# Merging the first self attention, the sign layer and the masked cross attention of a two-layer Perceiver kernel into one program, with batch 0 running ahead

## What is computed

```python
x = x + xattn0(layernorm(x), ctx)      # 16 heads of 64, rotary keys, scores clipped, 2048 context rows, bias bo
x = x + attn0(layernorm(x))            # causal self attention, 16 heads of 32, rotary q and k, biases bq bk bv bp
x = x + layernorm(x) @ sign(weight).T  # the sign layer
x = x + relu(xattn1(layernorm(x), ctx, ctx, mask) @ wo.T + wo_b)   # 16 heads of 32, additive mask
x = x + attn1(layernorm(x))            # causal self attention, 16 heads of 64
x = x + experts(layernorm(x))          # 8 experts, the best 2 per row
```

## Time and profile before

| | |
|---|---|
| three runs | 1287.05, 1293.71, 1293.89 us; median 1293.71 |
| the profiled execution | 1290.84 us, of which span 1289.1 us |
| TensorE matmul | 1206.2 us busy (94%) |
| VectorE | 679.2 us busy (53%) |
| ScalarE | 531.8 us busy (41%) |
| GpSimd | 219.6 us busy (17%) |
| mean granted TensorE clock | 0.967 |
| start of the last weighing in the rotary cross attention | 549.29 us |
| start of the steady part of the masked cross attention | 686.91 us |

### The profile page before, as it was taken

How to read it: one execution, slowest core, us unless ns; L and a number is a source line. 1 busy time by engine, 2 the same in 40 slices (tenths; PEclk the granted TensorE clock), 3 DMA queues, 4 the chain that set the end, 5 groups by cost and what they waited for, 6 DMA issues and landing times. The chain is left out here.

```text
span 1289.1 us, 23031 instructions
## 1 busy us (share of the span) xinstructions
PE 1206.2 (94%) x9696; PEld 959.9 (74%) x9696; DVE 679.2 (53%) x1179; ACT 531.8 (41%) x895; POOL 219.6 (17%) x181
## 2 busy tenths in 40 slices
PE   5899999999999999979647999899799999999998
PEld 4678888888788888735314666585689999999997
DVE  3555454545564533444447886304666656666663
ACT  2442323332433222204217998314454454444442
POOL 0143444444334443330000000001000000000000
PEclk9899999999999999989858999999799999999999
DMA  7110000010000010513131334210345544445540
GB/s 279 33 67 17 34 30 34 18 36 16 34 17 10 9 66 2 196 55 143 48 149 34 132 132 170 104 55 1 117 178 196 193 178 175 177 189 195 195 163 17
DMA packets 27874, 125.49 MB, mean 97 GB/s; under 512 B 2686, under 2 KB 2942, under 8 KB 17289
## 3 DMA queue, kind: packets, MB, share of 16 engines
q1 hardware_dynamic: 27784, 124.22, 25.4%
HBM read 123.68 MB, written 0.52 MB: 96 GB/s over the span
## 5 line engine op out<-in xcount | busy, mean ns | idle before, releaser
L631 POOL TENSOR_TENSOR norm_both<-norm_both,prob 128x512 f32<-128x512 f32 x120 | 156.8, 1307 | 149.9 <-DVE prob L440 142.3
L57 PE MATMUL mo_h_ps<-mo_x_hi,mo_w_hi 128*128 128x256 f32 x512 | 146.6, 286 | 2.1 <-DVE mo_x_lo L1661 2.1
L58 PE MATMUL mo_h_ps<-mo_x_lo,mo_w_hi 128*128 128x256 f32 x512 | 146.4, 286 | 0.0
L59 PE MATMUL mo_h_ps<-mo_x_hi,mo_w_lo 128*128 128x256 f32 x512 | 146.4, 286 | 0.0
L563 ACT ACTIVATE prob<-u_ps 128x512 f32<-128x512 f32 x128 | 66.1, 605 | 179.2 <-PE u_ps L717 179.2
L423 DVE TENSOR_TENSOR turned<-k_ps,tabs 128x512 f32<-128x512 f32 x32 | 22.1, 690 | 203.4 <-PE k_ps L59 203.4
L1615 DVE TENSOR_TENSOR mo_w_lo<-w_raw,mo_w_hi 128x2048 fp32r<-128x2048 f32 x32 | 73.3, 2292 | 73.7 <-ACT mo_w_hi L1564 73.7
L57 PE MATMUL k_ps<-ctx_hi,wk_hi 128*128 128x512 f32 x256 | 105.2, 411 | 3.7 <-DVE wk_lo L411 3.7
L57 PE MATMUL u_ps<-wv_hi,ctx_hi 128*128 128x512 f32 x256 | 103.0, 402 | 2.0 <-DVE wv_lo L405 1.3
L57 PEld LDWEIGHTS mo_h_ps<-mo_x_hi,mo_w_hi 128*128 128x128 f32 x512 | 99.8, 195 | 3.7 <-DVE mo_x_lo L1661 2.5
L59 PE MATMUL k_ps<-ctx_hi,wk_lo 128*128 128x512 f32 x256 | 102.3, 400 | 0.0
(11 more groups left out here) (260 smaller groups left out, 2313.8 us busy)
## 6 DMA issues: line engine op xcount, KB each, us to landing
w_raw<-in_w SPq DMA_DIRECT2D x64, 1024.0 KB, 6.0
ctx_raw<-in_ctx_rows SPq DMA_DIRECT2D x8, 1024.0 KB, 5.6
x_k<-in_ctx_T SPq DMA_DIRECT2D x8, 1024.0 KB, 7.0
x_val<-in_ctx_heads SPq DMA_DIRECT2D x8, 1024.0 KB, 4.8
tabs<-in_rot_tabs SPq DMA_DIRECT2D x8, 512.0 KB, 4.0
vals<-in_wq_rows SPq DMA_DIRECT2D x4, 512.0 KB, 7.2
ctx_raw<-in_wo SPq DMA_DIRECT2D x1, 2048.0 KB
x_mask<-in_mask SPq DMA_DIRECT2D x2, 1024.0 KB, 8.8
```

Source lines behind the costliest of these rows:

```text
L57: pe.matmul(out, w_hi, x_hi, start=start, stop=False)
L58: pe.matmul(out, w_hi, x_lo, start=False, stop=False)
L59: return pe.matmul(out, w_lo, x_hi, start=False, stop=stop)
L631: ins = pool.tensor_tensor(to, to, src, ALU.add)
```

## The change

- **Tail of the rotary block.** `bo` comes as 128 equal rows and is added to `resid` by VectorE at step 28. `project_out(0)` runs its products 0 to 4 ahead of the denominators of batch 1 and 5 to 7 behind them. Batch 1's denominators are inverted and multiplied in eight pieces of 128 columns, and each product of `project_out(1)` waits for its own piece. Between the pieces batch 0 is added to `resid` and its statistics are taken; normalising, transposing and storing batch 0's rows for the next layer also happens in this block. GpSimd prepares the rounded constants here.
- **One block `middle`** for self attention 0, sign layer and masked cross attention. `constant` is gone: `bp` comes as 128 rows and is added to `resid` by VectorE, `bv` is added when the weighed values are stored (`keep_out`). Normalisation is done per batch (`moments`, `centred`), and the sign layer and next normalisation of batch 0 stand between the pieces of batch 1. Two of batch 1's transposed pieces are stored by ScalarE, and three of its four divisions are VectorE's.
- **Fill.** For t < 7 each bank of `scores` waits for its own reading, and VectorE waits per bank, with one `gate` write each; the semaphore `score` counts banks in all steps. `scores(0)` stands behind the transposes of batch 1's normalised rows for the sign layer. `signs(4, 1)` and the normalisation of batch 1 stand between the first four steps.
- SyncE issues the keys, values and mask at the start of `middle`, the two weights of the second self attention after both outputs of self attention 0 are through (it waits for `y`), and the further keys behind these.
- Steps 7 to 39 of the masked cross attention, the second self attention and the experts have the same instructions in the same order, but for the rises of `score`.

```diff
 # cross_attention_rotary, VectorE
+                if t == 28:
+                    dve.wait_ge(s["bo_in"], 16)
+                    for b in range(NB):
+                        dve.tensor_tensor(resid[:, b, :], resid[:, b, :], bo[:], ALU.add).then_inc(s["bo_added"], 1)
...
-            for u in range(2):
-                dve.wait_ge(s["den_mm"], 2 + u + 1)
-                dve.reciprocal(den[:, u, :], u_ps[:, 2 + u, :]).then_inc(s["recip"], 1)
...
+            dve.wait_ge(s["weighed"], NT)
+            for k in range(8):
+                cols = slice((k % 4) * P, (k % 4) * P + P)
+                dve.wait_ge(s["den_mm"], 2 + k // 4 + 1)
+                dve.reciprocal(den[:, k // 4, cols], u_ps[:, 2 + k // 4, cols]).then_inc(s["recip"], 1)
+                dve.wait_ge(s["recip"], 2 + k + 1)
+                dve.tensor_tensor(attn_T[:, k, P:2 * P], o_ps[:, k // 4, cols], den[:, k // 4, cols],
                                   ALU.mult).then_inc(s["normalised"], 1)
+                if k == 3:
+                    add(0)
+                    dve.wait_ge(s["added"], 1)
+                    dve.bn_stats(ln_stats[:, 0, :], resid[:, 0, :]).then_inc(ln_s["ln_step"], 1)
+                elif k == 4:
...
 # cross_attention_rotary, TensorE
-            project_out(0)
+            project_out(0, range(5))
             pe.wait_ge(s["exped"], 4 * NT)
             denominators(1)
-            project_out(1)
+            project_out(0, range(5, 8))
+            project_out(1, range(8))
+            pe.wait_ge(ln_s["ln"], 1)
+            for k in range(KD):
+                ins = pe.transpose(u_ps[:, 0, k * P:(k + 1) * P], normed[:, 0, k * P:(k + 1) * P], ident[:])
 # middle, SyncE
+            sp.wait_ge(s["y"], NB)
+            for n in ("sa1_wq", "sa1_wk"):
+                sp.dma_start(env[n][:], rows(n)).then_inc(env["sa1_w_in"], 16)
+            load_keys(2)
 # middle, TensorE: scores(t), then the written order
-                if t >= 1:
-                    pe.wait_ge(s["masked"], 4 * t)
+                if t >= LAG:
+                    pe.wait_ge(x["masked"], 4 * t)
                 for a in range(4):
+                    if 1 <= t < LAG:
+                        pe.wait_ge(x["masked"], 4 * (t - 1) + a + 1)
...
-                ins.then_inc(s["score"], 1)
+                              stop=True).then_inc(x["score"], 1)
...
+            project_rows(0, 0)
+            project_rows(0, 1)
+            turn_norm(1, 1, 3)
+            project_rows(0, 2)
+            turn_rows(0)
+            project_rows(1, 0)
+            attend(0)
+            project_rows(1, 1)
+            project_rows(1, 2)
+            turn_rows(1)
+            for n in range(4):
+                turn_scores(0, n)
+            attend(1)
+            weigh_values(0)
+            project_values(0)
+            for n in range(4):
+                turn_scores(1, n)
+            turn_norm(2, 0, 3)
+            weigh_values(1)
+            signs(2, 0)
+            project_values(1)
+            turn_norm(3, 0, 3)
+            turn_norm(4, 1, 3)
+            pe.wait_ge(s["T_out"], 4)
+            scores(0)
+            scores(1)
+            signs(4, 1)
+            scores(2)
+            scores(3)
+            turn_norm(5, 1, 3)
 # middle, VectorE: the written order from batch 1's maxima on, then the masked reading
+            tops(1, 0)
+            tops(1, 1)
+            keep_out(0)
+            tops(1, 2)
+            tops(1, 3)
+            scaled(1, 0)
+            inverse(1, 1)
+            scaled(1, 2)
+            add_values(0)
+            moments(2, 0)
+            scaled(1, 3)
+            keep_turned(1, 0)
+            centred(2, 0)
+            keep_turned(1, 3)
+            keep_out(1)
+            add_signs(0)
+            moments(3, 0)
+            centred(3, 0)
+            add_values(1)
+            moments(4, 1)
+            centred(4, 1)
+            masked(0)
+            masked(1)
+            add_signs(1)
+            moments(5, 1)
+            masked(2)
+            centred(5, 1)
+            masked(3)
+            top(0)
...
                 for a in range(4):
+                    if t < LAG or a == 0:
+                        dve.wait_ge(x["score"], 4 * t + (a + 1 if t < LAG else 4))
+                        dve.memset(x_gate[0:1, t, a:a + 1], 0.0).then_inc(x["gate"], 1)
```

More of the change, by code:

```diff
@@ L804, in self_attention @@
     ln_stats, ln_mv, ln_var, ln_std, ln_rstd = (env["ln_" + n] for n in ("stats", "mv", "var", "std", "rstd"))
-    per = P // dh
-    KA = H // per
-    W = H * dh
-    NW = W // D
-    scale = dh ** -0.5 if layer == 0 else dh ** 0.5
-    wq, wk, wv, wp = (env[f"{tag}_{n}"] for n in ("wq", "wk", "wv", "wp"))
-    w_in, w_count = env[f"{tag}_w_in"], 10 if layer == 0 else 3
-    names = ["step", "var", "std", "ln", "T", "T_out", "rounded", "proj", "v_out", "qkT", "qkT_out", "score", "top",
-             "exped", "recip", "scaled_dve", "scaled_pool", "pT", "pT_out", "pv", "aT_dve", "aT_act", "y"]
@@ L814, in self_attention @@
[L814 to L836 removed]
+    KA, per, dh = 4, 4, DHS
@@ new lines, in middle @@
+    scale = dh ** -0.5
+    wq, wk, wv, wp = (env["sa0_w"][n] for n in ("wq", "wk", "wv", "wp"))
+    bv, bp, cos, sin = env["sa0_bv"], env["sa0_bp"], env["sa0_rc"], env["sa0_rs"]
+    ident_r, mask_r, ones_r, bias_r = (env["sa0_" + n] for n in ("ident_r", "mask_r", "ones_r", "bias_r"))
+    sgn_w, sa0_w_in = env["sgn_w"], env["sa0_w_in"]
+    s = {n: sem("sa0_" + n) for n in
+         ("bp_added", "proj", "v_out", "qkT", "qkT_out", "score", "top",
+          "exped", "recip", "scaled_dve", "scaled_pool", "pT", "pT_dve", "pT_act", "pv", "aT", "y", "added", "rope",
+          "signed", "sg_y", "sg_added")}
@@ new lines, in middle @@
+    s.update(env["ln_sem"])
+    x = {n: sem("x1_" + n) for n in
+         ("score", "gate", "masked", "top", "exped", "pT", "act_out", "dve_out", "pv", "den", "spread",
+          "wide", "wide_out", "normed", "y")}
+    w_in = sem("x1_wo_in")
+    s_k, s_v, s_m = ([sem(f"x1_{n}_in{r}") for r in range(2)] for n in "kvm")
+    NGRP = NB * 4
+    NST = NGRP * 4
+    LAG = 7
+    mine = lambda q: (1, 3) if q + LAG >= NST else (1,)
+    act_at, dve_at = {}, {}
+    for q in range(NST):
+        for a in range(4):
+            at = dve_at if a in mine(q) else act_at
+            at[q, a] = len(at) + 1
@@ L1489, in _ @@
+            for b in range(NB):
+                for n in range(4):
+                    tops(b, n)
+            for b in range(NB):
+                for n in range(4):
+                    scaled(b, n)
+            for b in range(NB):
+                for n in range(4):
+                    evacuate(b, n)
+            keep_out(0)
+            keep_out(1)
+            add(0)
             add(1)
```

1150 lines of the change are left out of this document (570 added, 580 removed).

## The result

The changed kernel takes 1257.41 us in the median of four runs (1255.41 to 1260.21), the kernel before 1292.17 (four runs, 1287.05 to 1293.89): a ratio of 0.9728, 95% interval 0.9704 to 0.9752, some 35 us faster. The forecast was 1251 with a range of 1244 to 1262. The profiled execution took 1257.47 us, of which 1255.7 are its span: 33.4 less than the span of before.

A forecast was written before the change was run, and what follows sets the result against it. Bound: a chain of waits from engine to engine in the rewritten stretch. 15.1 - 0.5 + 18.9 + 9.0 - 2.5 = 40.0 us off the profiled 1290.84 gives 1250.8, forecast 1251; own range 1244 to 1257, widened to 1244 to 1262.

The forecast's parts named there:

- First mark: End of the rotary block: first product of the first self attention moves from 585.44 to 570.35, 15.1 us gained.
- Second mark: Start of batch 0's output product, from 617.01 to 602.4: the gain becomes 14.6, 0.5 us less.
- Third mark: Start of scores(0), behind the joined layers: 18.9 us more gained, less 2.5 for one fall of the clock.
- The nearness of 1.85 to 2.28: Joined layers: TensorE's 1.85 us wait likened to an earlier 2.28 followed by clock 0.50; one fall, 2.5 us lost.
- Fourth mark: Start of scores(7), the fill's end: 24.45 us from scores(0) instead of 33.45 with banks freed singly, 9.0 gained.
- TensorE's loop at half clock: Fill: TensorE's loop per bank, 2.8 us at half clock, 1.8 at full, beside VectorE's step of 2.65.
- Behind it: From scores(7) to the end: the same 599.5 us of span as before, nothing gained or lost.
- (a): Rival: clock stays low through the joined layers, signs(2,0), project_values(1), signs(4,1) at half; 10.5 lost, not 2.5; 1259; chance 0.17.
- (b): Rival, fill: four heads' products freed singly run one behind another; 1261 us; chance 0.12; sign: VectorE gaps over 0.3.
- (c): Rival: the steady stage starts and stays at half clock; with thirteen slow steps 1304 us; chance 0.02.
- the rule on semaphore tails: Per-bank rises of score: 26.3 ns for each increment more, an estimated 2.5 us, sum 1253.3; not charged.
- Keys: Keys land 7.0 us after issue at 570, in time for scores(0); further keys needed only at 651: nothing lost.

The follow-up runs named there:

- signs spread: Changed kernel with signs(4,1) spread behind scores(0), (1) and (2), and VectorE reading step 2 ahead of add_signs(1): 1250.67 us, ratio to before 0.9663.
- coarse denominators: Changed kernel with batch 1's denominators in two 512-column pieces instead of eight, batch 0's addition and statistics behind: 1258.28 us; with signs spread too, 1253.70.
- the freed-alone version: Kernel before with only the fill's banks of scores freed singly, nothing else changed: 1285.71 us, ratio to before 0.9933.
- the last experiment: Changed kernel with signs spread, coarse denominators, unread products ahead of scores(0) and the last weighing, plus twelve unread full-array products ahead of scores(4): 1253.34 us.

## Why the prediction came out as it did

The direction and the method held: four marks on a chain of waits, 40.0 us foreseen and 33.4 had. The measured 1257.41 lies just beyond the forecast's own range, 1244 to 1257, and within 1244 to 1262 only because that was widened for the rivals. That the gain up to `scores(0)` was as foreseen is luck in part: a fall of the clock that was not counted (1.7) and a counted one that did not come (2.5) nearly cancel. The steps:

- **First mark, 15.1 foreseen, 13.2 had.** Each price in it was right, the 1.19 a piece among them. The mis-sized term is one that I had copied without thought: the last weighing, 1.97 in the earlier trace rows. The wait of 2.5 us ahead of it stands in ten of the twelve profiles, with and without the change, and in eight of those the clock fell behind it; it held in the one profile of before that I had, and in that of signs spread, where the first product came 21.36 behind the weighing's start, for 21.06 foreseen and 23.02 in the changed kernel. One profile shows one outcome of such a wait, not its price.
- **Second mark.** Right, to 0.1.
- **Third mark, 16.4 foreseen with the clock, 19.0 had.** The chain was right to 0.1: by its own working 18.9, without the clock's 2.5. The fall that I had put behind the 1.85 us ahead of `turn_scores(1,3)` (measured 1.62) did not come in the changed kernel's two profiles; of the ten of `middle` it came there in two, both with coarse denominators, and cost 1.6. The nearness of 1.85 to 2.28 was a weak ground.
- **Fourth mark, 9.0 foreseen, 2.7 had: the step that failed.** I had TensorE at full clock through the fill, because the bound of a step was VectorE's 2.65 and no wait was left. Three parts make the 6.3 us. From `scores(0)` to `signs(4,1)` 6.87 instead of 4.8, and `signs(4,1)` 5.36 instead of 3.5: 3.9 from the clock that fell behind the 2.50 us wait (with the wait filled they were 4.97 and 3.70), which I had not seen as one, though the chain (addition, `moments`, root, `centred`: 2.8 us of VectorE and ScalarE with TensorE idle) stood in my own third mark. From the end of the sign layer to `top` 0.5 was gained. From `top` to `scores(7)` 10.86 instead of 8.0: 1.48 of waiting ahead of `scores(4)`, three steps of 2.87 instead of 2.65 (0.7), and the transposes ahead of `scores(7)` at half clock. My own sum had 2.8 for TensorE's loop at half clock; what was wrong was to take the other figure.
- **Behind it, 0 foreseen, 1.1 lost:** `scores(7)` to `scores(8)` took 5.02 (655.14 to 660.16) instead of 3.89, with the clock low until 659. From `scores(8)` on both spans have 595.5 or 595.6; in the other ten profiles it is 595.8 to 598.9, so that equality is in part chance.
- **Rivals.** (a) had the right cause and mostly the wrong place: of its three products `signs(2,0)` and `project_values(1)` ran at 1.00, and `signs(4,1)` mostly at 0.50, which is the sign named for (a), and cost 1.9 of its 3.5. Its 1259 is nearer to the 1257.41 than my 1251, for another sum. The clock that 18 us of strips had not raised in the freed-alone version rose at about 685, behind the first transposes (680.40), with `scores(7)` between them. By the rule of the Trainium skill, TensorE: Matmul & The Clock Gate, Part 4, that transposes do not count as busy, they would have had no part in that; the trace disagrees as far as one such place can. (b) is refuted by 2.87 a step, although gaps of 0.31, just over the 0.3 that I had named as its sign, do stand at the borders of the steps: at half clock TensorE is the slower one. (c) did not come. The rise of `score` for every bank costs nothing that shows: TensorE's steady step is 4.13 before, with one rise a step (693.53 to 697.66), and after, with four (660.16 to 664.29), and the 2.47 of a step at full clock is below my 2.65. The 2.5 us of the rule on semaphore tails that I had set beside the sum were not needed to explain anything; in the fill no run isolates them.
- **Keys.** No wait for a DMA appeared between 570 and 660.

## What to carry to other kernels

Where a chain of short steps leaves TensorE idle for 1.6 to 2.5 us ahead of dense work, as here, price that work at both levels of the clock, and look at several profiles before taking one outcome as its price. Products that nobody reads, put into such a wait, paid here (3.3 to 3.9 us for 4.0 us of products that lay mostly in idle time), and so did cutting one dense layer into parts that fill the waits of the next stage (4.5 to 5 us, at most some 2 of it without the clock's help). Put into the strips of the steps 4 to 6, where TensorE was busy at half clock, such products only cost. Fine pieces are worth their overhead only if somebody waits for the first one: here the eight denominators lost 0.5.

## What the runs showed of the hardware

- TensorE counted as busy 2.00 of 2.00 us does not imply the upper clock. Products on 32-row strips, freed bank by bank, ran for 18.31 us at 0.50 (1.2 GHz) in the freed-alone version, and in the last experiment the clock fell from 1.00 (2.4 GHz) within such a run. Two full-array products in each of three steps did not lift it. The Trainium skill, TensorE: Matmul & The Clock Gate, section "Why this matters for your kernels", advises to keep TensorE busy continuously; here that alone was not enough. Whether it is the strips themselves, I have not shown: no run replaced them by full-array products of the same length.
- The same wait lets the clock fall in one execution and not in another: the 2.5 us at 549 in eight profiles of ten. The 2.5 us ahead of `scores(0)` did so in all six that have it, the 1.6 us at 610 in two of ten.
- Four strips whose banks come free 0.62 apart still overlap: eight pieces in 2.87 us at half clock, against 2.09 when all four are issued together.
